# Six adjacency blocks built ahead from the end of layer zero, and layer two's residual sums in turns with the split of the silu rows

## The chip, the core and the metric

The kernel runs on one core of one Trainium2 chip. The metric is the time of one execution on the device in microseconds. The engines are TensorE (PE, with its weight loads as PEld), VectorE (DVE), ScalarE (ACT), GpSimd (POOL) and SyncE (SP), which issues most of the transfers. Each has a queue of its own, works it off in order, and waits at semaphores for the others.

## The reference

Four graph layers over 3125 nodes of 128 features and 53125 edges, each followed by a residual sum and a normalisation of the rows:

```python
edge_index = jnp.stack([src, dst])
x = _layernorm(x + _L0(x, src, dst, ...))                        # attention, 4 heads
x = _layernorm(x + _L1(x, edge_index, W))                        # relu((H + segment_sum(H[src], dst)) @ W)
x = _layernorm(x + _L2(x, edge_index, edge_attr_4, ...))         # silu messages, edge weights, update net
x = _layernorm(x + _L3(x, edge_index, edge_type_64, ...))        # (x[src] + rel) @ W_msg.T, mean over dst
```

Layer one needs, for each node, the sum of its neighbours' rows. That is a product with the adjacency matrix, whose entry (source, destination) is the number of edges between the two.

## The kernel before

Nodes are cut into NB = 25 blocks of 128. Layer zero walks over NT = 650 tiles of 128 edges in NBATCH = 109 batches of six: TensorE gathers source rows through one-hot matrices, VectorE weights them (L1767), TensorE scatters them to the destinations (L2500). ScalarE copies the sums of a block from PSUM (L1194), and VectorE normalises.

Layer one makes the adjacency out of the same one-hot matrices. Its steps are numbered s = 0 to 174, s = q x 25 + b: b is a source block, q one of seven groups of destination blocks, four blocks (512 columns) wide for q = 0 to 3 and three (384 columns) for q = 4 to 6. For each step:

- VectorE writes one-hot rows of the sources into one of SBUF = 6 places (`set_hots`, L1950). The one-hot matrices of the destinations come from memory in chunks of five blocks (`hots_load`, L774), four chunks at a time in `big` and `XT`.
- TensorE multiplies them, `build(s)` (L2581 to L2591), into one of four PSUM banks (`adj_bank`). From s = 4 on it waits until the bank is free, that is until copy s-4 has been made.
- ScalarE copies the block to one of XBUF = 4 places of `adjf` in fp32r (L1286), once `apply1(s-4)` has released that place. We call it the wide copy. A second copy as bytes goes to memory for layer three: for s % 5 in 1, 3 VectorE makes it from `adjf` (L1965), for the others ScalarE makes it from PSUM (L1289).
- TensorE multiplies the rows of the nodes, in two parts `XH` and `XL`, with `adjf`: `apply1(s)` (L2611).

The order on TensorE is written out by hand: build(0), build(1), then for each even s build(s+2), build(s+3), apply1(s), apply1(s+1). Waits are on counts, so a queue stands at its first wait that isn't met. The waits that matter here are these (before, in `build` and in ScalarE's loop):

```python
if s >= 4:
    pe.wait_ge(adjf_cp, s - 3)          # wide copy s-4 made
    act_copied(pe, s - 4)               # ScalarE's byte copies up to s-4 made
...
act.wait_ge(adj_mm, s + 1)              # build(s) done
if s >= XBUF:
    act.wait_ge(applied, s - XBUF + 1)  # apply1(s-4) done
```

Between the layers, TensorE turns the counts of neighbours (`rc_tr`, L2552), ScalarE copies them (`crow`, L1269), SyncE stores them (L786), reads them back as a broadcast of 1600 KB (L788), and only then issues the loads of chunks two and three. The rows of layer one's input are scaled by ScalarE (L1227) and VectorE, and parted into `XH` (ScalarE, L1255) and `XL` (VectorE, L1983).

Layer two begins with dense products in seven banks of four blocks: messages (Wagg), residual (Wres, semaphore `xr`) and the first part of the update net (`upx`, L2670). The silu rows `T1` are parted into three bf16 parts for the gathers: ScalarE copies the top part (L1246), VectorE takes the rest (L1944), ScalarE copies the middle part (L1249), VectorE takes the low part (L1940). Then VectorE adds the residual to the bias (L2006), which frees the banks in PSUM for `upx`, and ScalarE adds the bias to `upx` (L1308). The gathers (`gather2`, L2688) wait for all seven.

Of the kernel before, what the change touches and what calls it, by code (L numbers as in the profile page):

```python
# [13 lines left out]
P = 128  # L14
F = 128
# [32 lines left out]
def gnn_kernel(nc, ins, out):  # L48
# [113 lines left out]
    def up2_at(i):  # L162
        return up_at(i) + 4

# [45 lines left out]
    with ctx:  # L210
# [491 lines left out]
        def _(sp):  # L702
# [77 lines left out]
            for r in range(3):  # L780
                sp.wait_ge(hots_out[r], hots_stored(r))
# [13 lines left out]
            for n in range(BANKS * NCK):  # L795
                q, c = n // NCK, n % NCK
                if n == 0:
                    sp.wait_ge(hots_wide, NBATCH)
                    hots_load(2)
                    hots_load(3)  # L800
# [10 lines left out]
                if c == 1 and q:  # L811
                    rel_store(q - 1)
# [213 lines left out]
        def _(act):  # L1026
# [169 lines left out]
            for k in range(NBATCH):  # L1196
# [5 lines left out]
                own_values(k)  # L1202
                if k + 1 < NBATCH:
                    hots_widened(k + 1, 0)
# [37 lines left out]
            def split(n, src, ready):  # L1242
                for i in range(BANKS + 1):
                    if i < BANKS:
                        ready(i)
                        C.copy(XP[:, nodes(i), 0, :], src[:, nodes(i), :]).then_inc(xp_top, 1)  # L1246
                    if i:
                        act.wait_ge(xp_rest, BANKS * n + i)
                        C.copy(XP[:, nodes(i - 1), 1, :], AG[:, cols(i - 1)].rearrange("p (b f) -> p b f", f=F)).then_inc(xp_mid, 1)  # L1249

            C.copy(SLc[:, 1, :, :], SLc[:, 0, :, :]).then_inc(pairs_ready, 1)

# [3 lines left out]

            for h in range(2):
                deviations(1, h)
            act.wait_ge(scale_ready, 1)
# [9 lines left out]
            C.copy(crow[:, :], bank(7)[0:NB, 0:P]).then_inc(rc_cp, 1)  # L1269
# [8 lines left out]
            for q in range(BANKS):  # L1278
                w = even_width(q)
                for b in range(NB):  # L1280
                    s = q * NB + b
                    act.wait_ge(adj_mm, s + 1)
                    if s >= XBUF:
                        act.wait_ge(applied, s - XBUF + 1)
                        dve_copied(act, s - XBUF)
                    C.copy(adjf[:, s % XBUF, 0:w], adj_bank(s)[:, 0:w]).then_inc(adjf_cp, 1)  # L1286
                    if not by_dve(s):
                        adj_free(act, s)
                        C.copy(adj_slot(s), adj_bank(s)[:, 0:w]).then_inc(adj_act, 1)  # L1289
                    if q == 0 and b % 2 == 0 and HBANK - 1 + b // 2 < BANKS:  # L1290
                        round_rows(1, HBANK - 1 + b // 2)
                    if q and b == 9:
                        rel_rows(q - 1)
# [9 lines left out]
            split(1, T1, lambda i: act.wait_ge(silu2, i + 1))  # L1303
            act.wait_ge(rows2_out, 16 * BANKS)
            for i in range(BANKS):
# [149 lines left out]
        def _(dve):  # L1455
# [196 lines left out]

            dve.wait_ge(pool_consts, 8)
# [97 lines left out]
            for k in range(NBATCH):  # L1751
# [11 lines left out]
                if k + 1 < NBATCH:  # L1763
# [5 lines left out]
                                va[:, :, :, F:ROW0].unsqueeze(4).to_broadcast([P, a, n // a, H, FH]), ALU.mult).then_inc(vals_ready, 1)  # L1769
                for i in range(BANKS):  # L1770
# [125 lines left out]
            def normalise(n, dst, *steps):  # L1896
# [40 lines left out]
            def split(n, src):  # L1937
                def low(i):
                    dve.wait_ge(xp_mid, BANKS * (n - 1) + i + 1)
                    V.tensor_tensor(XP[:, nodes(i), 2, :], AG[:, cols(i)].rearrange("p (b f) -> p b f", f=F), XP[:, nodes(i), 1, :], ALU.subtract).then_inc(xp_low, 1)  # L1940

                for i in range(BANKS):
                    dve.wait_ge(xp_top, BANKS * n + i + 1)
                    V.tensor_tensor(AG[:, cols(i)].rearrange("p (b f) -> p b f", f=F), src[:, nodes(i), :], XP[:, nodes(i), 0, :], ALU.subtract).then_inc(xp_rest, 1)  # L1944
# [901 lines left out]
```

## Time and profile before

| | us |
|---|---|
| median of 3 runs | 1089.12 |
| lowest and highest | 1088.42, 1090.14 |
| profiled execution | 1089.84 |
| its span from first to last instruction | 1088.0 |
| TensorE busy | 1002.6 (92%) |
| VectorE busy | 861.1 (79%) |
| ScalarE busy | 691.3 (64%) |
| GpSimd busy | 218.2 (20%) |

The profile is one execution. A view by stretch gives each engine's busy time in a part of the span, and the clock that TensorE was granted as a share of 2.4 GHz. A view in order of time gives start, duration, engine, line and operation, out<-in, a count of merged instructions, and in brackets the idle time of the engine before it with what ended it. PE's durations overlap, since products are pipelined: the distance from start to start tells how long one holds the engine.

### The profile page before, as it was taken

Reading aid. Unit: us, or ns where it says so; the run is one execution under the profiler, and the core shown is the slowest. Engines: PE = TensorE matmul, PEld = TensorE weight load, DVE = VectorE, ACT = ScalarE, POOL = GpSimd, SP = SyncE. Lnnn points to the kernel's source line nnn. Section 1 sums busy time; section 2 is a strip of 40 time slices with the busy share of each in tenths; the row PEclk is TensorE's granted clock in tenths of the full one; section 3 lists DMA queues with packets and bytes.
Section 4 is the critical chain, followed back from the end, with each engine's and each line's share of the span. In section 5 each row is a group of like instructions: output and inputs, shape, how many; then the busy total and the mean of one; then the engine's idle time right before and its main releaser. Section 6 shows DMA issues by size and latency. Waiting matters only on the chain.

```text
span 1088.0 us, 27899 instructions
## 1 busy us (share of the span) xinstructions
PE 1002.6 (92%) x10463; PEld 874.7 (80%) x10463; DVE 861.1 (79%) x1934; ACT 691.3 (64%) x1489; POOL 218.2 (20%) x260
## 2 busy tenths in 40 slices
PE   3798979699999999995999999779999999989997
PEld 3343557599999999995788889669999999976775
DVE  6875999988998989987766677788787888766754
ACT  3467765454555555456888888577677776776554
POOL 4501340000000000000000000126666666610000
PEclk9899999899999999997999999889999999999998
DMA  6000020366767677752866564235444445334232
GB/s 159 1 2 1 4 68 3 121 207 225 238 215 225 222 238 227 204 175 72 292 195 193 172 201 141 82 104 140 138 136 129 131 131 139 109 112 124 69 99 82
DMA packets 86925, 150.38 MB, mean 138 GB/s; under 512 B 14524, under 2 KB 58375, under 8 KB 86557
## 3 DMA queue, kind: packets, MB, share of 16 engines
q1 hardware_dynamic: 65609, 116.01, 35.9%
q10 hardware_dynamic: 16122, 22.16, 5.7%
q0 software_dynamic: 5056, 10.36, 3.9%
q8 instruction: 88, 1.44, 0.5%
q14 instruction: 50, 0.40, 0.1%
HBM read 112.56 MB, written 35.94 MB: 136 GB/s over the span
## 4 chain that ended last, share of the span: by engine, by line
PE 81%; DVE 10%; ACT 4%; issue 3%; DMA 2%; POOL 0%; POOLq 0%; DVEq 0%; SPq 0%; ACTq 0%
PE PS L2500 14%; PE PS L2705 14%; PE PS L2488 11%; PE PS L2688 8%; PE PS L2611 7%; PE PS L2791 6%; PE PS L2581 3%; PE PS L2588 3%; PE PS L2326 2%; PE PS L2339 2%; DVE ring L1659 2%; DVE vo L1663 2%; PE PS L2403 2%; ACT X L1227 1%; PE PS L2357 1%
## 5 line engine op out<-in xcount | busy, mean ns | idle before, releaser
L1151 ACT CAST vo<-XT 128x768 f32<-128x768 bf16 (+1 forms) x218 | 180.3, 827 | 163.7 <-PE PS L2705 64.2
L984 POOL DMA_INDIRECT XT<-tab,ring x158 | 159.9, 1012 | 113.5 <-PE PS L2705 60.2
L2500 PE MATMUL PS<-vo 128*128 128x133 f32 x1300 | 175.9, 284 | 1.2 <-ACT vo L1151 1.2
L2500 PEld LDWEIGHTS PS<-vo 128*128 128x128 f32 x1300 | 157.2, 191 | 1.4 <-issue 1.4
L2488 PE MATMUL PS<-kp,ring 128*128 128x132 bf16 x1950 | 146.7, 221 | 3.2 <-DVE ring L1631 1.7
L2705 PE MATMUL PS<-vo 128*128 128x128 f32 x984 | 132.8, 279 | 0.0
L2488 PEld LDWEIGHTS PS<-kp,ring 128*128 128x128 bf16 x1950 | 125.6, 97 | 5.4 <-DVE ring L1631 1.8
L1641 DVE TENSOR_TENSOR XT<-iotab,XT 128x768 bf16<-128x768 bf16 (+1 forms) x218 | 120.0, 551 | 3.2 <-DMA hots_d<-XT 1.5
L2705 PEld LDWEIGHTS PS<-vo 128*128 128x128 f32 x984 | 118.9, 191 | 3.0 <-issue 2.4
L2490 PE MATMUL PS<-SDP,ring 128*128 128x12 bf16 x650 | 110.2, 170 | 0.0
L1286 ACT CAST adjf_r<-PS 128x512 fp32r<-128x512 f32 (+1 forms) x175 | 92.4, 550 | 25.4 <-PE PS L2581 23.6
L1631 DVE TENSOR_SCALAR ring<-ring,pcolm 128x1664 bf16<-128x1664 bf16 x146 | 91.2, 652 | 18.9 <-PE PS L2688 15.5
L1767 DVE TENSOR_TENSOR vo<-PS,vo 128x768 f32<-128x768 f32 (+1 forms) x109 | 103.2, 947 | 0.7 <-ACT vo L1201 0.5
L2107 DVE TENSOR_TENSOR vo<-PS,EWS 128x640 f32<-128x640 f32 (+2 forms) x109 | 82.3, 755 | 27.1 <-PE PS L2688 26.9
L2688 PE MATMUL PS<-kp,ring 128*128 128x128 bf16 x1476 | 99.9, 219 | 0.8 <-ACT big L1308 0.8
L965 POOL IOTA ring<- 128x650 int32 x1 | 0.8, 759 | 477.5 <-PE PS L2588 477.5
L2688 PEld LDWEIGHTS PS<-kp,ring 128*128 128x128 bf16 x1476 | 91.3, 98 | 2.3 <-ACT big L1308 1.0
L1950 DVE TENSOR_TENSOR ring<-IN,SLc 128x768 bf16<-128x768 bf16 x182 | 91.4, 550 | 0.0
L2791 PE MATMUL PS<-adjf_r,xh_r 128*128 128x512 f32 (+1 forms) x175 | 70.6, 404 | 7.2 <-DVE adjf_r L2255 3.4
L2611 PE MATMUL PS<-adjf_r,xh_r 128*128 128x512 f32 (+1 forms) x175 | 72.9, 417 | 0.0
L1103 ACT ACTIVATE kp<-PS 128x512 f32<-128x512 f32 x104 | 57.6, 608 | 23.0 <-PE PS L2326 22.1
L2611 PE MATMUL PS<-adjf_r,xl_r 128*128 128x512 f32 (+1 forms) x175 | 65.3, 373 | 0.0
(350 smaller groups left out, 2008.6 us busy)
## 6 DMA issues: line engine op xcount, KB each, us to landing
ring<-rows_d SPq DMA_DIRECT2D x146, 416.0 KB, 5.8
hots_d<-XT ACTq DMA_DIRECT2D x108, 192.0 KB, 4.7
big<-hots_d SPq DMA_DIRECT2D x10, 640.0 KB, 5.3
XT<-hots_d SPq DMA_DIRECT2D x10, 640.0 KB, 4.8
adj_d<-ring SPq DMA_DIRECT2D x20, 320.0 KB, 2.4
big<-hots_d SPq DMA_DIRECT2D x8, 480.0 KB, 4.4
adj_d<-ring SPq DMA_DIRECT2D x15, 240.0 KB, 2.1
ring<-adj_d SPq DMA_DIRECT2D x11, 320.0 KB, 3.0
```

Of the source, the lines that this page charges most:

```text
L984: G.indirect_dma_start(far_rows[:, f % FBUF, :], None, tab[2], bass.IndirectOffsetOnAxis(ap=far_row[:, t:t + 1], axis=0)).then_inc(far_in[ ...
L1151: C.copy(ohd[:, k % 3, 0:n, :], ohb[:, k % 3, 0:n, :]).then_inc(hots_wide, 1)
L1286: C.copy(adjf[:, s % XBUF, 0:w], adj_bank(s)[:, 0:w]).then_inc(adjf_cp, 1)
L1641: V.tensor_tensor(ohb[:, k % 3, 0:n, :].rearrange("p t (h d) -> p t h d", d=2), iotab[:, :].rearrange("p (h d) -> p h d", d=2).unsqueeze(1 ...
L1767: V.tensor_tensor(va[:, :, :, 0:F].rearrange("p a i (h f) -> p a i h f", h=H), gathered(k, 0, F).rearrange("p a i (h f) -> p a i h f", h=H ...
L2488: T.matmul(PS[:, to:to + ROW0], ohT[:, 0, h % OBUF, l * P:(l + 1) * P], KP[:, source(t), part, :], start=part == 0, stop=part == 2)
L2490: T.matmul(PS[:, to + ROW0:to + ROW0 + 3 * H], ohT[:, 1, h % OBUF, l * P:(l + 1) * P], SDP[:, t // JN, :, :].rearrange("p t h -> p (t h)") ...
L2500: T.matmul(bank(6 + b % 2)[:, 0:VW], ohd[:, k % 3, i, :], vals[:, k % 3, i, :], start=j == 0, stop=j == JN - 1).then_inc(scattered, 1)
L2611: o = T.matmul(to[:, 0:w], xs[:, b, :], adjf[:, s % XBUF, 0:w], start=b == 0 and part == 0, stop=False, skip_group_check=True)
L2688: o = T.matmul(PS[:, to:to + F], ohT[:, 0, h % OBUF, l * P:(l + 1) * P], XP[:, source(t), part, :], start=part == 0, stop=part == 2)
L2705: T.matmul(bank(6 + q % 2)[:, (b % 4) * P:(b % 4 + 1) * P], rows_of(k, i, t), ohd[:, k % 3, i, :], start=j == 0, stop=j == JN - 1).then_in ...
L2791: o = T.matmul(to[:, 0:w], xs[:, b, :], adjf[:, s % XBUF, 0:w], start=b == 0 and part == 0, stop=False, skip_group_check=True)
```

## The change

One piece is layer one's start and the distance between building and applying. The one-hot rows of blocks 0 to 5 and of the diagonal are written in layer zero's last batches, from batch 103 on (EARLY_HOTS, AHEAD = 6). TensorE builds blocks 0 to 3 as soon as layer zero's last sums are copied, turns the counts into bank 4 instead of bank 7, builds blocks 4 and 5, and from then on builds s+6 and s+7 before it applies s and s+1. XBUF and the four PSUM banks are as before. ScalarE makes the first four wide copies before the normalisation and its byte copies of them between the standard deviations and the scaling of the rows. SyncE issues the loads of chunks zero and one earlier; those of chunks two and three stay behind `crow`. VectorE's byte copies follow set_hots at a distance of six instead of four, and the relation sums move three blocks later.

The other piece is in layer two: VectorE's residual sums (L2006) stand in turns with its split steps, and ScalarE's `upx` copies in turns with its own.

```diff
+    EARLY_HOTS = HT * (NU - 1) // BT - 3
+    AHEAD = 6
...
             for r in range(3):
-                sp.wait_ge(hots_out[r], hots_stored(r))
+                sp.wait_ge(hots_out[r], 16 * len(range(r, (len(even(0)) * JN - 1) // BT + 1, 3)))
             extra_load(0)
             hots_load(0)
             hots_load(1)
...
+            def block_wide(s):
+                w = even_width(s // NB)
+                act.wait_ge(adj_mm, s + 1)
+                if s >= XBUF:
+                    act.wait_ge(applied, s - XBUF + 1)
+                    dve_copied(act, s - XBUF)
+                C.copy(adjf[:, s % XBUF, 0:w], adj_bank(s)[:, 0:w]).then_inc(adjf_cp, 1)
+
+            def block_byte(s):
+                if not by_dve(s):
+                    adj_free(act, s)
+                    C.copy(adj_slot(s), adj_bank(s)[:, 0:even_width(s // NB)]).then_inc(adj_act, 1)
+
+            for s in range(XBUF):
+                block_wide(s)
             for h in range(2):
                 deviations(1, h)
+            for s in range(XBUF):
+                block_byte(s)
             act.wait_ge(scale_ready, 1)
...
             act.wait_ge(rc_tr, 1)
-            C.copy(crow[:, :], bank(7)[0:NB, 0:P]).then_inc(rc_cp, 1)
+            C.copy(crow[:, :], bank(4)[0:NB, 0:P]).then_inc(rc_cp, 1)
...
+            for i in range(BANKS + 3):
+                if i < BANKS:
+                    act.wait_ge(silu2, i + 1)
+                    C.copy(XP[:, nodes(i), 0, :], T1[:, nodes(i), :]).then_inc(xp_top, 1)
+                if 0 < i <= BANKS:
+                    act.wait_ge(xp_rest, BANKS + i)
+                    C.copy(XP[:, nodes(i - 1), 1, :], AG[:, cols(i - 1)].rearrange("p (b f) -> p b f", f=F)).then_inc(xp_mid, 1)
+                if i >= 3:
+                    hidden_start(i - 3)
...
+                if k == EARLY_HOTS:
+                    dve.wait_ge(pairs_ready, 3)
+                    set_hots(0, NB, ohx[:, 0, :])
+                if 0 <= k - EARLY_HOTS < AHEAD:
+                    set_hots(0, k - EARLY_HOTS, ohs[:, k - EARLY_HOTS, :])
...
-                    set_hots(0, NB, ohx[:, 0, :])
...
-                    set_hots(q, b, ohs[:, s % SBUF, :])
-                    if s >= 4:
-                        adj_copy(s - 4)
+                    if s >= AHEAD:
+                        set_hots(q, b, ohs[:, s % SBUF, :])
+                    if s >= AHEAD:
+                        adj_copy(s - AHEAD)
...
+            for i in range(BANKS + 2):
+                if i < BANKS:
+                    rest_of(i)
+                if 0 < i <= BANKS:
+                    low_of(i - 1)
+                if i >= 2:
+                    residual(i - 2)
...
-                if s == 3:
-                    pe.wait_ge(rc_cp, 1)
+                if s == 0:
+                    pe.wait_ge(vals_ready, NBATCH)
+                    pe.wait_ge(sums_cp, NB)
...
-            build(0)
-            build(1)
+            for s in range(XBUF):
+                build(s)
+            pe.wait_ge(cnt_ready, 1)
+            T.transpose(bank(4)[0:NB, 0:P], rc[:, :], ident[:, :]).then_inc(rc_tr, 1)
+            for s in range(XBUF, AHEAD):
+                build(s)
             for s in range(0, NS, 2):
-                for n in (s + 2, s + 3):
+                for n in (s + AHEAD, s + AHEAD + 1):
                     if n < NS:
                         build(n)
                 for n in (s, s + 1):
```

TensorE at the start of layer one, before: the end of build(2), build(3), and the first apply. `rc_cp` is the count copied by ScalarE.

```order
L2588 MATMUL PS<-ring,big 128x64 x4
L2581 MATMUL PS<-big,ring 128x128 [waits rc_cp,ohs_ready]
L2581 MATMUL PS<-big,ring 128x128 x3
L2584 MATMUL PS<-big,ring 128x128
L2588 MATMUL PS<-ring,big 128x64 x4
L2611 MATMUL PS<-adjf_r,xh_r 128x512 [waits adjf_cp,xp_rest]
L2611 MATMUL PS<-adjf_r,xl_r 128x512
```

The same place now: build(3), the transposed counts, build(4), build(5) and the first product of build(6); build(7), apply1(0) and apply1(1) come behind it.

```order
L2607 MATMUL PS<-big,ring 128x128 [waits ohs_ready]
L2607 MATMUL PS<-big,ring 128x128 x3
L2610 MATMUL PS<-big,ring 128x128
L2614 MATMUL PS<-ring,big 128x64 x4
L2653 MATMUL PS<-ident,rc 25x128 [waits cnt_ready]
L2607 MATMUL PS<-big,ring 128x128 [waits adj_act,adjf_cp,ohs_ready]
L2607 MATMUL PS<-big,ring 128x128 x3
L2614 MATMUL PS<-ring,big 128x64 x4
L2607 MATMUL PS<-big,ring 128x128 [waits adj_act,hots_got1,adjf_cp,ohs_ready]
```

The first apply stands behind eight builds instead of four, and the builds from the fifth on wait for ScalarE's copies (`adjf_cp` the wide ones, `adj_act` the byte ones).

ScalarE between the layers, before: `SLc` is copied, then the normalisation, the count row and the first wide and byte copy.

```order
L1251 COPY SLc<-SLc 128x728
L1223 ACT_TABLE_LOAD
L1223 ACTIVATE rstd<-mb,eps 128x16 [waits var_ready]
L1223 ACTIVATE rstd<-mb,eps 128x9 [waits var_ready]
L1227 ACTIVATE X<-big,shift,rstd 128x128 [waits scale_ready]
```

ScalarE between the layers, now:

```order
L1260 CAST adjf_r<-PS 128x512 [waits adj_mm] x4
L1231 ACT_TABLE_LOAD
L1231 ACTIVATE rstd<-mb,eps 128x16 [waits var_ready]
L1231 ACTIVATE rstd<-mb,eps 128x9 [waits var_ready]
L1265 CAST ring<-PS 128x512 x2
L1235 ACTIVATE X<-big,shift,rstd 128x128 [waits scale_ready]
```

Four wide copies stand ahead of the normalisation and two byte copies inside it; the copy of `SLc` is in layer zero's batch 101.

ScalarE in layer two's preparation, before (L1246 top part, L1249 middle part, L1308 the update net's bias):

```order
L1246 CAST kp<-big 128x4x128 [waits silu2]
L1249 CAST kp<-big 128x4x128 [waits xp_rest]
L1246 CAST kp<-big 128x128 [waits silu2]
L1249 CAST kp<-big 128x4x128 [waits xp_rest]
L1249 CAST kp<-big 128x128 [waits xp_rest]
L1308 ACTIVATE big<-PS,bu 128x512 [waits xp_rest,upx,rows2_out]
```

The same place now (L1322 top, L1325 middle, L1317 bias):

```order
L1325 CAST kp<-big 128x4x128 [waits xp_rest]
L1317 ACTIVATE big<-PS,bu 128x512 [waits xp_rest,upx,rows2_out]
L1322 CAST kp<-big 128x4x128 [waits silu2]
L1325 CAST kp<-big 128x4x128 [waits xp_rest]
L1317 ACTIVATE big<-PS,bu 128x512 [waits xp_rest,upx]
```

The bias steps moved from behind all copies to one behind each pair of copies, and each waits for TensorE (`upx`).

## Rows read from the trace of the kernel before

**Rows 1.** Busy time by stretch: PE, PEld, DVE, ACT, POOL, granted clock, DMA share, GB/s.

```profile
499.80:510.10 10.30, 0.59 (x2) 0.20 (x2) 8.49 (x40) 6.74 (x15) 0.00 (x0) 0.76 0.32 113
524.80:680.00 155.20, 155.07 (x1618) 132.12 (x1619) 108.18 (x241) 127.40 (x277) 0.76 (x1) 1.00 0.63 193
```

**Rows 2.** Order of time, TensorE, the first block and build(10).

```profile
509.80 0.39 PE L2560 MATMUL PS<-zeros 1*128 1x256 bf16 x1 [5.33 <-DVE ring L1950]
...
524.93 0.39 PE L2581 MATMUL PS<-XT,ring 128*128 128x128 bf16 x4 [0.17 <-DMA XT<-hots_d]
```

**Rows 3.** Order of time, TensorE and ScalarE, a pair of steps with 512 columns.

```profile
601.30 0.48 PE L2611 MATMUL PS<-adjf_r,xh_r 128*128 128x512 f32 x1
601.31 0.59 ACT L1289 CAST ring<-PS 128x512 uint8<-128x512 f32 x1
...
601.78 0.60 ACT L1286 CAST adjf_r<-PS 128x512 fp32r<-128x512 f32 x1
601.85 0.39 PE L2611 MATMUL PS<-adjf_r,xh_r 128*128 128x512 f32 x1
...
602.08 0.40 PE L2611 MATMUL PS<-adjf_r,xl_r 128*128 128x512 f32 x1
...
602.31 0.41 PE L2581 MATMUL PS<-big,ring 128*128 128x128 bf16 x4
...
602.76 0.59 ACT L1286 CAST adjf_r<-PS 128x512 fp32r<-128x512 f32 x1 [0.38 <-PE PS L2581]
602.79 0.41 PE L2581 MATMUL PS<-big,ring 128*128 128x128 bf16 x4
...
603.24 0.48 PE L2611 MATMUL PS<-adjf_r,xh_r 128*128 128x512 f32 x1
```

**Rows 4.** The same view, a pair of steps with 384 columns.

```profile
674.00 0.36 PE L2581 MATMUL PS<-big,ring 128*128 128x128 bf16 x3
...
674.36 0.35 PE L2581 MATMUL PS<-big,ring 128*128 128x128 bf16 x3
674.40 0.86 ACT L1286 CAST adjf_r<-PS 128x384 fp32r<-128x384 f32 x2 [0.18 <-PE PS L2581]
...
674.70 0.42 PE L2611 MATMUL PS<-adjf_r,xh_r 128*128 128x384 f32 x1
...
675.13 0.34 PE L2611 MATMUL PS<-adjf_r,xh_r 128*128 128x384 f32 x1
...
675.14 0.50 ACT L1289 CAST ring<-PS 128x384 uint8<-128x384 f32 x1
...
675.31 0.33 PE L2611 MATMUL PS<-adjf_r,xl_r 128*128 128x384 f32 x1
...
675.48 0.36 PE L2581 MATMUL PS<-XT,ring 128*128 128x128 bf16 x3
```

**Rows 5.** One line's instructions, ScalarE's wide copy: shortest, median, longest ns, forms.

```profile
L1286 ACT CAST adjf_r<-PS x175: 473/585/623, 514.5 to 679.0; 128x512 fp32r<-128x512 f32 x100, 128x384 fp32r<-128x384 f32 x75
```

**Rows 6.** The page's group of set_hots; order of time, ScalarE's scaling and SyncE's load.

```profile
L1950 DVE TENSOR_TENSOR ring<-IN,SLc 128x768 bf16<-128x768 bf16 x182 | 91.4, 550 | 0.0
...
506.29 3.18 ACT L1227 ACTIVATE X<-big,shift,rstd 128x128 f32<-128x128 f32 x8 [0.53 <-DVE shift L1916]
...
516.32 0.98 SPq L774 DMA_DIRECT2D XT<-hots_d  x2
```

**Rows 7.** Order of time, layer two's preparation: VectorE's residual sums, last bias steps, first gather.

```profile
715.43 3.87 DVE L2006 TENSOR_TENSOR big<-PS,bu 128x512 f32<-128x512 f32 x7
...
723.60 0.94 ACT L1308 ACTIVATE big<-PS,bu 128x512 f32<-128x512 f32 x2 [0.17 <-PE PS L2670]
...
724.60 3.19 PE L2688 MATMUL PS<-kp,ring 128*128 128x128 bf16 x54 [0.82 <-ACT big L1308]
```

**Rows 8.** Busy time by stretch, columns as in rows 1: TensorE with pauses, and idle.

```profile
147.00:160.00 13.00, 9.23 (x107) 8.41 (x104) 11.44 (x16) 7.55 (x22) 9.10 (x11) 1.00 0.48 137
711.30:716.10 4.80, 0.00 (x0) 0.00 (x0) 4.80 (x11) 3.10 (x7) 0.00 (x0) 0.71 0.00 0
```

More of the change, by code:

```diff
@@ L798, in _ @@
                     sp.wait_ge(hots_wide, NBATCH)
+                    for r in range(3):
+                        sp.wait_ge(hots_out[r], hots_stored(r))
                     hots_load(2)
@@ L810, in _ @@
                     extra_load(q + 1)
-                if c == 1 and q:
+                if c == 2 and q:
                     rel_store(q - 1)
@@ L1202, in _ @@
                 own_values(k)
+                if k == EARLY_HOTS - 2:
+                    C.copy(SLc[:, 1, :, :], SLc[:, 0, :, :]).then_inc(pairs_ready, 1)
                 if k + 1 < NBATCH:
@@ L1240, in copy_xt @@
                     C.copy(XT[:, cols(i)], PS[:, cols(i)]).then_inc(xt_act, 1)
[L1242 to L1251, printed above, removed]
             def round_rows(n, i):
@@ L1281, in _ @@
                     s = q * NB + b
-                    act.wait_ge(adj_mm, s + 1)
                     if s >= XBUF:
[L1284 to L1289, printed above, removed]
+                        block_wide(s)
+                        block_byte(s)
                     if q == 0 and b % 2 == 0 and HBANK - 1 + b // 2 < BANKS:
                         round_rows(1, HBANK - 1 + b // 2)
-                    if q and b == 9:
+                    if q and b == 12:
                         rel_rows(q - 1)
@@ L1302, in _, with hidden_start @@
                 C.activation(T1[:, nodes(i), :], NX[:, nodes(i), :], ACT.Silu).then_inc(silu2, 1)
-            split(1, T1, lambda i: act.wait_ge(silu2, i + 1))
-            act.wait_ge(rows2_out, 16 * BANKS)
-            for i in range(BANKS):
+            def hidden_start(i):
+                if i == 0:
+                    act.wait_ge(rows2_out, 16 * BANKS)
                 act.wait_ge(upx, i + 1)
@@ L1651, in _, with set_hots @@
             FIRST = [h for h in units_at(0) if HT * h < 2 * BT]
+            def set_hots(q, j, buf):
+                V.tensor_tensor(buf.rearrange("p (k n b) -> p k n b", k=3, b=4), IN1[:, :, :].rearrange("p (k n) b -> p k n b", k=3),
+                                SLc[:, :, j, 4 * q:4 * q + 4].unsqueeze(2).to_broadcast([P, 3, NREL, 4]), ALU.is_equal).then_inc(ohs_ready, 1)
             dve.wait_ge(pool_consts, 8)
@@ L1935, in copy_xt @@
                     V.tensor_copy(XT[:, cols(i)], PS[:, cols(i)]).then_inc(xt_dve, 1)
[L1937 to L1944, printed above, removed]
-                    if i:
-                        low(i - 1)
-                low(BANKS - 1)
-            def set_hots(q, j, buf):
-                V.tensor_tensor(buf.rearrange("p (k n b) -> p k n b", k=3, b=4), IN1[:, :, :].rearrange("p (k n) b -> p k n b", k=3),
-                                SLc[:, :, j, 4 * q:4 * q + 4].unsqueeze(2).to_broadcast([P, 3, NREL, 4]), ALU.is_equal).then_inc(ohs_ready, 1)
-            dve.wait_ge(pairs_ready, 3)
             normalise(1, X)
@@ L2605, in apply1 @@
                     pe.wait_ge(crel_cp, q - 1)
+                if b == 0 and q == 1:
+                    pe.wait_ge(rc_cp, 1)
                 if q == 0:
```

20 lines of the change are left out of this document (12 added, 8 removed).

## The prediction

> **What bounds the kernel now.** I read the page's busy times, then the table of busy time by stretch, then the order of time around the three places that the diff touches. TensorE bounds it. From 524.8 to 680.0 us, which is nearly all of layer one's product with the adjacency, TensorE is busy 155.07 of 155.20 us at full clock [rows 1]. That stage has no slack: whatever makes TensorE wait there lengthens the kernel. The slack lies beside it: 10.3 us with almost no TensorE work between layer zero and the first block [rows 1, 2], and layer two's preparation, where the projections end 0.8 us before the first gather [rows 7].
>
> In the full stage each pair of steps is build(s+2), build(s+3), apply1(s), apply1(s+1). With 512 columns a pair takes 601.30 to 603.24, 1.94 us: the first apply 0.55, the second 0.46, the builds 0.48 and 0.45 [rows 3]. With 384 columns it takes 674.00 to 675.48, 1.48 us: the second build 0.34, the first apply 0.43 [rows 4]. ScalarE's copies never hold TensorE up here, because the block that is to be copied was applied long ago.
>
> **The distance of six.** This is the term that decides. Nothing is added to TensorE's work, but the builds stand six blocks ahead of the applies instead of two, and both rings keep four places. Follow an even n. build(n) waits until block_wide(n-4) has emptied its PSUM bank. block_wide(n-4) waits until apply1(n-8) has released its place in `adjf`. With distance two TensorE has applied up to n-3 when it reaches build(n): five applies lie between apply1(n-8) and it. With distance six it has applied up to n-7: apply1(n-8) is the last but one instruction group on the same queue, and only apply1(n-7), 0.46 us, stands between. So a turn TensorE, ScalarE, TensorE comes into every pair, and the engine that was full waits in it.
>
> The turn, 512 columns, counted from the point where apply1(n-8) has been issued:
> - its last product ends 0.17 us later (602.08 + 0.40 against the next group's 602.31), and ScalarE starts 0.04 us after a product's end (602.31 + 0.41, then 602.76) [rows 3]: 0.21 us;
> - block_wide(n-4), then block_byte(n-4): ScalarE goes from one to the next in 0.47 us (601.31 to 601.78) [rows 3]: 0.94 us for both;
> - block_wide(n-3), which build(n+1) waits for, whole: 0.60 us [rows 3];
> - back to TensorE: 0.06 us (the last activation ends at 723.60 + 0.94, the gather starts at 724.60) [rows 7];
> - build(n+1), the second of its pair, 0.45, and apply1(n-6), the first of its, 0.55 us [rows 3], and the turn is closed.
>
> That is 0.21 + 0.94 + 0.60 + 0.06 + 1.00 = 2.81 us. Of the five kinds of pair by s % 5 (bytes of s % 5 in 0, 2, 4 are ScalarE's, the rest VectorE's), four have one byte copy in this chain and one has two, which makes 3.28 us. Where the one byte copy belongs to the second block it stands behind block_wide(n-3), and the sum is the same. The mean is (4 x 2.81 + 3.28) / 5 = 2.90 us, 0.96 us over 1.94. It holds from build 10 to build 99, 45 pairs: **43.2 us**.
>
> With 384 columns: 0.16 + 0.04 (675.31 + 0.33 against 675.48), copies 0.37 apart (674.40 with two copies, then 675.14), the wide copy 0.49 (the two take 0.86), 0.06, build 0.34, apply 0.43 [rows 4]. That is 0.20 + 0.74 + 0.49 + 0.06 + 0.77 = 2.26 us, 2.63 with two bytes, mean 2.33: 0.85 us over 1.48. Blocks 100 to 174 (100 wide copies of 512 columns, 75 of 384 [rows 5]) are 37.5 pairs: **31.9 us**. TensorE waits for about a third of the stage (1 - 1.94 / 2.90); VectorE and the loads have more room than before, so nothing else becomes late.
>
> At a boundary of two column groups TensorE's extra products partly fill a wait, and ScalarE's two small copies of the relation sums, hidden now, come into the chain. I set these off against each other and keep 3 us both ways.
>
> **The start of layer one.** The six set_hots of the first blocks, 0.55 us each [rows 6], and the one for the diagonal move into the last batches of layer zero, where VectorE has idle time between batches; only the last two stand before the last sums, up to 1.1 us on the chain into the normalisation, and one (0.5) leaves it. Builds 0 to 3 now run at 500 us instead of from 509.80 [rows 2]. But two byte copies (0.94 us) stand in front of ScalarE's row scaling, which had 0.53 us of idle time before 506.29 [rows 6]. Together `crow` comes about 1.1 - 0.5 + 0.94 later, 1.5 us. That matters through SyncE's queue: the loads of chunks two and three still stand behind `crow`'s store, and the first one ends the wait at 524.93 [rows 2, 6]. build(10) needs it. In the order of before TensorE has then done applies 0 to 7; in the new order apply1(4) stands behind build(10), so only 0 to 3. The head start therefore ends in a longer wait for the same transfer: 1.5 us later, and four applies owed, which at the end, at 384 columns, cost about 4 x 0.39 = 1.6 us. **+3.1 us**; bounds 0 (crow not later, the applies inside later waits) to 6. The early load of chunks zero and one costs nothing: their queue waits for nothing that is late.
>
> **Layer two.** The seven residual sums (715.43, 3.87 us [rows 7]) are spread among the split steps. VectorE's total is the same, so its last sum still ends near 719.3. A last narrow projection and activation need about 1 us more, so the gather can start at 720.3 at the best, 4.3 us before 724.60 [rows 7]. But on ScalarE the activation of bank i-3 now stands ahead of the silu copy of bank i+1, which VectorE's next split step waits for: projection, activation, copy, three VectorE steps of 0.55 to 0.6 and the handoffs close a round of about 4.4 us for two banks. From a first sum at 710.8 that gives the last activation at 722.8, or 724.5 if the clock is low in it. I take **-1.5 us**; bounds -4.3 and 0.
>
> The rest (`SLc`'s copy, the later place of relation rows, PSUM bank 4 for the count row) lies beside busy TensorE: 0.
>
> **Sum.** 1089.84 (profiled) + 43.2 + 31.9 + 3.1 - 1.5 = 1166.5. The median of the runs is 0.7 below the profiled one: 1165.8, say 1166 us.
>
> **Rivals.**
> A, the clock also falls. At half clock a pair costs TensorE at most twice 1.94, 3.9 us, against 2.90; half of the stage so is about (3.9 - 2.90) x 22 + (2.96 - 2.33) x 19 = 34 us more: 1200. Against it: from 147 to 160 us TensorE worked with pauses, busy 9.23 of 13 us, and the clock stayed full (mean 1.00), while it fell in the idle time from 711.3 to 716.1 (mean 0.71) [rows 8]; the new stage has work for 1.94 of 2.90 us and 1.48 of 2.33, in pauses of about half a microsecond. The Trainium skill (TensorE: Matmul & The Clock Gate, section "A second HAM failure mode: psum-queue depth-cycling") says that short idle times between groups of products, while PSUM banks are cycled in each iteration, make the clock swing between its two levels; by that rule this rival is the likelier one, by the rows the full clock. 6%.
> B, the turn is shorter by one copy, because ScalarE's byte copies find a place outside the chain: 0.47 x 45 + 0.37 x 37.5 = 35 us less, 1131. Against it: the queue is in order and build(n) waits for the byte of n-4 or its predecessor. 5%.
> C, faster: the turn is hidden as it was before. It decides at one point, whether a wide copy and a byte copy fit behind one apply of 0.46 us; they need 1.3. If they did, TensorE would stand five builds and two applies further when `crow` is written, 5 x 0.48 + 2 x 0.46 = 3.3 us, and with layer two's 1.5 the time is 1084. For it speaks only that ScalarE is busy 127.40 of 155.20 us [rows 1], so it has room in sum. 2%. With the late load (+3.1 - 1.5) the same hidden turn gives 1091, no difference: 2%.
>
> **How the numbers follow.** Forecast 85%, A 6%, B 5%, C 2% and 2%. Within the forecast a tenth of a microsecond more or less in each of the 82 turns is 8 us, and the other bounds are 3 and 4 us: 1153 to 1181, with 80% of the chance inside. 0.2%, 2.2 us, is about what a measurement of this kernel tells from no change: faster 0.02, same 0.02, slower 0.96.
>
> **What would show it.** Right: TensorE's builds wait for the wide or byte copy, some 0.9 us a pair from the first block to the last, the stage from build 10 to the last apply lasts about 230 us instead of 155, granted clock 1.00 in it, ScalarE's wide copies waiting for applies rather than builds; the load of chunk two lands at about 526 with TensorE idle before it. Wrong: pairs still near 1.94 us (C), 2.4 (B) or a clock under 0.9 there (A); a first gather more than 4 us nearer to the end of layer one than now.

## The result, and the profile after

The changed kernel takes 1178.24 us, median of 4 runs (1175.88 to 1181.61). The kernel before, run beside it, takes 1089.63 us (1088.42 to 1091.07). The ratio is 1.081, with a 95% interval of 1.080 to 1.083. The forecast was 1166, with a range of 1153 to 1181: slower, by the mechanism named, 12 us too little.

The profiled execution of the changed kernel took 1175.88 us, with a span of 1174.1 against 1088.0. Four moments, read from TensorE's order of time in both traces, divide the 86.1 us between them:

| stretch | before, us | after, us | difference |
|---|---|---|---|
| start to build(10) | 524.93 | 527.49 | +2.6 |
| build(10) to the last products of layer one (first `identr` product) | 155.2 | 239.2 | +84.1 |
| from there to layer two's first gather | 44.5 | 42.2 | -2.3 |
| first gather to the end | 363.4 | 365.2 | +1.8 |

So the full stage has nearly the whole loss. This is the table of busy time by stretch of the changed kernel, with the columns of [rows 1]: first TensorE's wait before build(10), then a short stretch behind it, then the stage whole and one piece of it.

```profile
523.70:527.40 3.70, 0.00 (x0) 0.00 (x0) 1.96 (x4) 1.33 (x4) 0.00 (x0) 1.00 0.93 303
528.20:531.60 3.40, 3.14 (x20) 2.18 (x17) 1.13 (x4) 1.48 (x3) 0.00 (x0) 0.55 1.03 358
531.60:766.00 234.40, 171.92 (x1595) 131.09 (x1596) 106.39 (x237) 128.55 (x276) 1.67 (x3) 1.00 0.40 121
...
600.00:660.00 60.00, 43.77 (x409) 32.39 (x406) 26.16 (x57) 32.53 (x64) 0.00 (x0) 1.00 0.41 125
```

Before, TensorE was busy 155.07 of 155.20 us [rows 1]; now it is busy 171.92 of 234.40, at the same granted clock of 1.00. (The busy time grew though the work didn't: before a pause the end of the last product, 0.16 us, is no longer covered by a next one, which is one reason why the waits below add up to less than 84 us.) Its waits in the stage, summed from 527 to 767 us (engine, line, what it waited for: us in total, times, longest), and the group of ScalarE's wide copy from the page (busy, mean ns, idle time before it and its releaser):

```profile
PE PS L2607 <- ACT ring L1265: 48.6, 80, 0.8
PE PS L2607 <- issue: 7.7, 26, 0.3
PE PS L2607 <- DVE ring L1673: 5.9, 14, 1.1
PE PS L2607 <- DMA XT<-hots_d: 3.8, 1, 3.8
```

```profile
L1260 ACT CAST adjf_r<-PS 128x512 fp32r<-128x512 f32 (+1 forms) x175 | 92.8, 547 | 114.5 <-PE PS L2607 100.1
```

Eighty waits of builds (L2607) for ScalarE's byte copy (L1265), and ScalarE's wide copy (L1260) in its turn 100.1 us idle for TensorE: each waits for the other. One such turn in the order of time, the columns being start, duration, engine and line, with idle time and releaser in brackets. It answers to [rows 3].

```profile
644.72 0.39 PE L2607 MATMUL PS<-big,ring 128*128 128x128 bf16 x4 [0.83 <-ACT ring L1265]
...
645.17 0.41 PE L2607 MATMUL PS<-big,ring 128*128 128x128 bf16 x4
...
645.62 0.47 PE L2639 MATMUL PS<-adjf_r,xh_r 128*128 128x512 f32 x1
645.93 0.39 PE L2639 MATMUL PS<-adjf_r,xl_r 128*128 128x512 f32 x1
646.16 0.40 PE L2639 MATMUL PS<-adjf_r,xh_r 128*128 128x512 f32 x1
646.41 0.58 ACT L1260 CAST adjf_r<-PS 128x512 fp32r<-128x512 f32 x1 [1.34 <-PE PS L2607]
646.89 0.59 ACT L1265 CAST ring<-PS 128x512 uint8<-128x512 f32 x1
647.36 0.60 ACT L1260 CAST adjf_r<-PS 128x512 fp32r<-128x512 f32 x1
647.62 0.39 PE L2607 MATMUL PS<-big,ring 128*128 128x128 bf16 x4 [0.83 <-ACT ring L1265]
...
648.07 0.24 PE L2607 MATMUL PS<-big,ring 128*128 128x128 bf16 x1
...
648.58 0.47 PE L2639 MATMUL PS<-adjf_r,xh_r 128*128 128x512 f32 x1
```

The first apply's last product ends at 646.32 (645.93 + 0.39), ScalarE starts at 646.41, its byte copy ends at 647.48, TensorE's first build starts at 647.62 and its second at 648.07. From build to build it is 2.90 us, where [rows 3] had 1.94. The bracket at ScalarE's wide copy names the build L2607 as what it waited for, but that build had been done long ago; the wide copy waits for the apply as well, and starts 0.09 us behind its end. Such a bracket has to be read with the ends of the rows around it.

### The profile page after: what moved, and what is told of

Read it like the earlier page. It is cut to its first block and busy times, and to the rows that moved or that the text cites. A ratio compares the mean times of both kernels' runs of the same rounds, so it can differ in the third digit from the quotient of the medians.

```text
span 1174.1 us, 27901 instructions
## 1 busy us (share of the span) xinstructions
PE 1018.9 (87%) x10463; PEld 872.3 (74%) x10463; DVE 861.4 (73%) x1934; ACT 692.7 (59%) x1489; POOL 218.6 (19%) x260
## 5 line engine op out<-in xcount | busy, mean ns | idle before, releaser
L1157 ACT CAST vo<-XT 128x768 f32<-128x768 bf16 (+1 forms) x218 | 180.3, 827 | 165.3 <-PE PS L2737 64.1
L1260 ACT CAST adjf_r<-PS 128x512 fp32r<-128x512 f32 (+1 forms) x175 | 92.8, 547 | 114.5 <-PE PS L2607 100.1
L1660 DVE TENSOR_TENSOR XT<-iotab,XT 128x768 bf16<-128x768 bf16 (+1 forms) x218 | 119.9, 551 | 1.6 <-DMA hots_d<-XT 0.8
L1975 DVE CAST ring<-adjf_r 128x512 uint8<-128x512 f32 (+1 forms) x70 | 27.8, 397 | 124.6 <-ACT adjf_r L1260 124.6
L1650 DVE TENSOR_SCALAR ring<-ring,pcolm 128x1664 bf16<-128x1664 bf16 x146 | 91.4, 654 | 18.8 <-PE PS L2720 15.7
```

The source lines that it names most:

```text
L1157: C.copy(ohd[:, k % 3, 0:n, :], ohb[:, k % 3, 0:n, :]).then_inc(hots_wide, 1)
L1660: V.tensor_tensor(ohb[:, k % 3, 0:n, :].rearrange("p t (h d) -> p t h d", d=2), iotab[:, :].rearrange("p (h d) -> p h d", d=2).unsqueeze(1 ...
```

## Experiments

Ten kernels were run. Beside each median stands the ratio to the kernel before, which ran on the same chip beside them (1090.05 us, 1089.75 and 1090.05 in the three groups).

### Distance four instead of six

```diff
-    AHEAD = 6
+    AHEAD = 4
```

> The changed kernel with AHEAD = 4 instead of 6, everything else kept (builds 0 to 3 early, the early set_hots, layer two's new order). Theory (the turn TensorE, ScalarE, TensorE comes from the distance of six on rings of four places): between apply1(n-8) and build(n) TensorE now has apply1(n-7), two builds and two applies, some 2.4 us of work against a turn of about 1.3 to 1.8 us on ScalarE, so nothing waits: stage from build 10 to the last apply about 156 us, pairs 1.94 us. Total 1089.6 + 2.6 (crow and with it the load of chunk two later) + 0.8 (two applies owed at that load) - 1.5 to -2.4 (layer two) = about 1091, 1088 to 1094. Rival 1 (the waits come from the moved set_hots, the new bank or the early blocks, not from the distance): stays above 1150. Rival 2 (each step away from distance two costs in proportion): about 1130.

Measured: 1092.99 us (10 runs, 1091.71 to 1094.74), ratio 1.0029 (1.0017 to 1.0041). One number takes 85 us off. Busy time by stretch of this kernel, and its build(10):

```profile
524.00:681.00 157.00, 157.00 (x1620) 133.45 (x1621) 106.81 (x237) 126.99 (x277) 1.09 (x3) 0.99 0.62 191
```

```profile
524.00 0.42 PE L2607 MATMUL PS<-XT,ring 128*128 128x128 bf16 x4 [3.17 <-DMA XT<-hots_d]
```

The stage has no wait, so the distance is the cause, and it doesn't act in proportion: at four the turn is hidden, at six it isn't. The 2.9 us left over the kernel before are no turns. The start has one part of them, with the wait of 3.17 us for chunk two; layer two's part is told below.

### The distance alone, in the kernel before

```diff
-            build(0)
-            build(1)
+            for s in range(6):
+                build(s)
             for s in range(0, NS, 2):
-                for n in (s + 2, s + 3):
+                for n in (s + 6, s + 7):
...
-                    if s >= 4:
-                        adj_copy(s - 4)
+                    if s >= 6:
+                        adj_copy(s - 6)
```

(The small copies moved with it as in the changed kernel: places 8, 12 and 2 instead of 5, 9 and 1; so did VectorE's parting of the later rows into `XL`.)

> The kernel before with the distance alone: TensorE builds six blocks ahead, VectorE's byte copies and the small copies stand where the changed kernel has them for that distance; start of layer one, bank 7 for the count row and layer two as before. Theory (distance): stage from build 10 to the last apply 84 us longer as in the changed kernel, four applies owed at the load of chunk two (+1.6), crow not later: 1089.6 + 84 + 1.6 = 1175, 1166 to 1184. Rival (the loss sits in the early start and its queue order): under 1110.

Measured: 1177.61 us (4 runs, 1175.29 to 1178.81), ratio 1.080 (1.078 to 1.083). The distance alone gives the whole loss, with layer zero's end and layer two as before. Together with the first run this excludes the moved set_hots, the new bank and the early blocks as a cause.

### ScalarE's byte copies out of the turn

```diff
         def by_dve(s):
-            return s % 5 in (1, 3)
+            return True
```

> The changed kernel with all byte copies on VectorE (by_dve true for every block), distance six kept. Theory (the turn's length is the sum of ScalarE's copies in it): 1.2 byte copies on average leave each turn, 0.47 us with 512 columns and 0.37 with 384: 0.56 x 45 + 0.44 x 37.5 = 42 us less, 1136 us, 1126 to 1146; pairs about 2.46 us with 512 columns, all alike. VectorE then has 2 x (0.55 + 0.43) = 1.96 us a pair. Rival (VectorE's set_hots, six places in a ring that TensorE empties six ahead, sets the pace): VectorE's added work lengthens the pair, 1178 or more.

Measured: 1134.39 us (4 runs), ratio 1.040 (1.038 to 1.043); 44 us less than the changed kernel, expected were 42. Distance six is kept, VectorE has more work than in the changed kernel, and yet the time falls. TensorE in the order of time:

```profile
622.93 0.39 PE L2607 MATMUL PS<-big,ring 128*128 128x128 bf16 x4 [0.35 <-ACT adjf_r L1260]
625.36 0.39 PE L2607 MATMUL PS<-big,ring 128*128 128x128 bf16 x4 [0.34 <-ACT adjf_r L1260]
```

The pair is 2.43 us, and it waits for the wide copy now: summed from 527 to 724 us TensorE's builds wait 19.7 us for it and 3.1 us for VectorE's one-hot rows. The turn's length is the sum of ScalarE's copies in it plus the handoffs, as the prediction had it; VectorE's ring of `ohs` is not what sets the pace.

### Distance six, one block at a time

```diff
-            for s in range(0, NS, 2):
-                for n in (s + AHEAD, s + AHEAD + 1):
+            for s in range(NS):
+                for n in (s + AHEAD,):
                     if n < NS:
                         build(n)
-                for n in (s, s + 1):
+                for n in (s,):
```

> The changed kernel, distance six kept, but TensorE's steps go one by one, build(s+6), apply1(s), instead of two builds and two applies. Theory (a chain TensorE, ScalarE, TensorE that closes over the queue order): now build(n-1) and apply1(n-7), 0.95 us, stand between apply1(n-8) and build(n), and the chain advances two steps in 0.24 + 0.47 + 0.60 + 0.14 + 0.45 + 0.55 = 2.45 us where the block's byte copy is ScalarE's (three blocks of five) and in 1.98 where it isn't, mean 2.26 against the 3.04 of a pair in the changed kernel (2.93 and 3.48 measured): 0.78 x 45 = 35 us less; with 384 columns 1.97 and 1.60, mean 1.82 against 2.44 (2.35 and 2.82 measured): 23 us less. 1178 - 58 = 1120, 1108 to 1135, since even and odd chains share ScalarE. Rival (only the number of blocks ahead counts against the rings of four, not the order in which they are issued): 1175 or more.

Measured: 1125.71 us (4 runs), ratio 1.033 (1.031 to 1.035): 52.5 us less than the changed kernel, expected were 58. In the order of time two steps with ScalarE's byte copy in them take the 2.45 us that were worked out:

```profile
622.43 0.39 PE L2607 MATMUL PS<-big,ring 128*128 128x128 bf16 x4 [0.29 <-ACT ring L1265]
...
623.42 0.25 PE L2607 MATMUL PS<-big,ring 128*128 128x128 bf16 x1
...
624.88 0.28 PE L2607 MATMUL PS<-big,ring 128*128 128x128 bf16 x2 [0.23 <-ACT ring L1265]
```

The number of blocks ahead is as before, and the rings have their four places. Only the order on TensorE's queue changed, and more than half of the loss went. The distance does its harm through what stands on the queue between apply1(n-8) and build(n): nothing but one apply in the changed kernel, a build and an apply here, and at distance four three applies and two builds.

### Layer two's new order alone

The kernel before with `rest_of`, `low_of`, `residual` and `hidden_start` in turns, as the diff of the change has them.

> The kernel before with the new order of layer two's split alone. In the changed kernel the stretch from the last apply to the first gather became 2.3 us shorter (42.2 against 44.5), and the stretch from the first gather to the end 1.8 us longer. Theory (a part is given back, because the load of the next row block is issued as late as before and the gathers now wait for it): first gather 2 to 2.5 us earlier, total only 0.4 to 1.0 us less, 1088.6 to 1089.2. Rival (the 1.8 us given back belong to something else in the changed kernel): total 2 to 2.5 us less, 1087.2.

Measured: 1090.48 us (12 runs, 5 rounds), ratio 1.0003 (0.9990 to 1.0015). No gain; the expected part of a microsecond isn't seen. Where it goes is read from three moments of each profiled execution, in us behind the first `identr` product of the last column group, with the duration of TensorE's last six projections (of the kernel before all fourteen stand in one group of 7.62 us):

| kernel | first gather | first scatter | last six projections |
|---|---|---|---|
| before | 44.5 | 47.7 | |
| changed | 42.2 | 47.1 | 2.23 |
| distance four (e1) | 43.2 | 48.2 | 2.23 |
| layer two alone (e3) | 44.3 | 47.7 | 3.90 |
| layer two with early one-hots (e6, below) | 42.1 | 45.3 | 2.23 |

From the first scatter to the end of the span every one of these executions takes 360.2 to 360.4 us. So the first scatter counts, and not the first gather, which the prediction looked at. In the changed kernel's profiled execution the first scatter came 0.6 us earlier, in that of e3 not at all. In the changed kernel, VectorE, SyncE's queue and TensorE:

```profile
806.79 1.20 DVE L1650 TENSOR_SCALAR ring<-ring,pcolm 128x1664 bf16<-128x1664 bf16 x2
...
807.45 4.73 SPq L744 DMA_DIRECT2D ring<-rows_d  x3
...
811.09 0.75 DVE L1650 TENSOR_SCALAR ring<-ring,pcolm 128x1664 bf16<-128x1664 bf16 x1 [3.10 <-DMA ring<-rows_d]
811.76 1.02 DVE L1660 TENSOR_TENSOR XT<-iotab,XT 128x768 bf16<-128x768 bf16 x2
...
813.80 1.58 PE L2737 MATMUL PS<-vo 128*128 128x128 f32 x12 [1.72 <-DVE vo L2134]
```

VectorE's first two one-hots of the edges (L1650) stand behind the last residual sum. The first of them frees a place for the third row block, which SyncE then loads; VectorE waits 3.10 us for it, the one-hots of destinations (L1660) stand behind that, and the first scatter at the end. In the kernel before the same wait was there, hidden behind the projections and ScalarE's copy of the slots:

```profile
723.67 0.65 DVE L1631 TENSOR_SCALAR ring<-ring,pcolm 128x1664 bf16<-128x1664 bf16 x1 [3.25 <-DMA ring<-rows_d]
725.74 1.04 DVE L1641 TENSOR_TENSOR XT<-iotab,XT 128x768 bf16<-128x768 bf16 x2 [1.42 <-ACT XT L1141]
```

The new order brings the projections forward but VectorE's last sum not, and so the load now ends last.

### The first edge one-hots early

```diff
             copy_xt(1)
+            edge_hots(0, 0, 1)
             for i in range(BANKS):
                 dve.wait_ge(mm2, i + 1)
...
+            edge_hots(1, 0, 1)
...
-            for h in units_at(0):
+            for h in units_at(0)[2:]:
                 edge_hots(h, 0, 1)
```

> The kernel of e3_before_layer2, with VectorE's first two edge one-hots of layer two put ahead of its additions of bagg and ahead of the split, where it waits for other engines (1.15 and 1.21 us). The load of the third row block, which waits for the first of them, then lands before 715 instead of 726. Theory (in e3 VectorE's third edge one-hot waits for this load, the one-hots of destinations wait behind it, and the first scatter behind them): the wait at 726.07 goes; what is next is ScalarE's copy of the slots, which ends at 726.4 in e3, so the first scatter comes 0.3 us earlier where TensorE's last projections run at the low clock (1.12 us became 3.90 for six), and 1.9 us earlier where they run at the full one: total 1090.2 or 1088.6, no more than 1091. Rival (layer two's start is bound elsewhere, the moved one-hots delay the residual sums): 1091 or more.

Measured: 1089.55 us (11 runs, 1087.3 to 1090.95), ratio 0.9996 (0.9987 to 1.0005). The wait for the load is gone and the first scatter follows the gather without one:

```profile
719.84 0.65 DVE L1641 TENSOR_SCALAR ring<-ring,pcolm 128x1664 bf16<-128x1664 bf16 x1
...
723.09 1.03 DVE L1651 TENSOR_TENSOR XT<-iotab,XT 128x768 bf16<-128x768 bf16 x2 [2.60 <-ACT XT L1141]
...
725.14 1.58 PE L2733 MATMUL PS<-vo 128*128 128x128 f32 x12
```

What ends last is ScalarE's copy of the slots (L1141), as expected, and behind it TensorE's projections. The profiled execution had the projections at the full clock and its scatter 2.4 us earlier; over all runs 0.2 us is left against the kernel before, where e3 was 0.4 above the one beside it, and neither is told from no change. This profiled execution was also the fastest of its eleven, and the clock in the projections is one thing that sets it apart from e3's: the same six take 2.2 us with a granted clock of 1.00 (this kernel) or 3.9 with 0.61 (e3). Both rows are from busy time by stretch, the first of this kernel, the second of e3:

```profile
718.00:722.00 4.00, 2.29 (x7) 1.03 (x8) 2.49 (x6) 2.54 (x6) 0.00 (x0) 1.00 0.07 27
```

```profile
720.60:725.00 4.40, 3.90 (x6) 1.60 (x6) 2.23 (x6) 1.39 (x3) 0.00 (x0) 0.61 0.37 88
```

TensorE had worked in short groups with the same waits, of up to 1.46 us, between them before either. e4 and e8 have this preparation too, and their six projections took 3.9 us like e3's. e8 differs from e7 in layer one's distance alone; its first scatter came 47.5 us behind the `identr` product, e7's 46.2. In e7 the low clock (0.57 from 712.0 to 715.6 us) fell on the four projections before, and the last six ran at 1.00 in 2.21 us. So the low stretch comes in one traced execution and not in another, and at different places, and what it costs depends on the place.

### The loads ahead of `crow`'s store

At distance four:

```diff
             hots_load(1)
+            sp.wait_ge(hots_wide, NBATCH)
+            for r in range(3):
+                sp.wait_ge(hots_out[r], hots_stored(r))
+            hots_load(2)
+            hots_load(3)
             sp.wait_ge(rc_cp, 1)
```

The same lines go from their old place behind the store.

> The kernel of e1_after_dist4 with SyncE's two loads of chunks two and three (and the waits for their data) put ahead of the wait for crow and its store. In e1 TensorE stood 3.17 us for that load (to 524.00) and then worked about 3 us at the low clock (builds and applies of 524.46 to 527.6 take 1.3 to 1.6 times as long, about 1 us). Theory (the load behind crow's store is what the early blocks run into): it lands before TensorE wants it, so 3.2 + 1.0 less: 1093.0 - 4.2 = 1088.8, 1087.5 to 1090.5, just below the kernel before. Rival (ScalarE's row scaling and rounding are late there as well, and take the wait over): 1092 to 1093, with a wait for ScalarE or VectorE of some 3 us in its place.

Measured: 1088.58 us (12 runs), ratio 0.9992 (0.9983 to 1.0002): by the medians 4.4 us less than e1 (4.1 by the ratios to the kernel before beside each), expected were 4.2. TensorE's build(10) follows its apply without a wait:

```profile
523.27 0.40 PE L2638 MATMUL PS<-adjf_r,xl_r 128*128 128x512 f32 x1
523.51 0.41 PE L2606 MATMUL PS<-XT,ring 128*128 128x128 bf16 x4
```

The same edit at distance six:

> The changed kernel, distance six kept, with SyncE's loads of chunks two and three ahead of crow's store. In the changed kernel TensorE waited 3.83 us for this load (to 527.49), and its clock was low again from 528.2 to 531.6. Theory (this wait is a term of its own beside the turns, as at distance four, where the same edit took 4.4 us off): 3.8 + 0.7 = 4.5 us less, 1173.7, 1172 to 1175.5. Rival (at distance six the turns take it over, since the blocks that stood ready are few): 1176 to 1178.

Measured: 1173.56 us (4 runs, 1171.36 to 1176.28), ratio 1.076 (1.075 to 1.078). By the medians 4.7 us less than the changed kernel, as the theory has it; but in the profiled executions build(10) comes 3.5 us earlier (counted from layer zero's last group of sums) and the stage's end only 1.9 us. The intervals of the two ratios don't overlap, so a gain is there. But this profiled execution is the slowest of its four and the changed kernel's the fastest, and from the first scatter to the end it took 362.0 us where the others in the table above took 360.3. Whether the turns take over part of the wait stays open.

### Both repairs together

On the changed kernel: TensorE four ahead (e7) or two ahead (e8), VectorE's six early set_hots kept, the loads ahead of `crow`'s store, the first two edge one-hots early, VectorE's byte copies four blocks behind again, and ScalarE's later byte copy behind `crow`:

```diff
-            for s in range(XBUF):
-                block_byte(s)
+            block_byte(0)
...
             C.copy(crow[:, :], bank(4)[0:NB, 0:P]).then_inc(rc_cp, 1)
+            for s in range(1, XBUF):
+                block_byte(s)
```

> Both repairs together, on the changed kernel: TensorE four ahead, VectorE's six early set_hots kept (so builds 4 and 5 need not wait for the seventh operation), loads of chunks two and three ahead of crow's store, ScalarE's byte copy of block 2 behind crow instead of ahead of the row scaling, the first two edge one-hots of layer two early. Theory: e1's 1093.0 less 4.2 (load), 0.5 (byte copy), 1.9 (row load of layer two at full clock) = 1086.4, 1084.5 to 1088.5, a little faster than before. Rival (the start of layer one is bound by ScalarE from 504 to 521 us, whatever TensorE has ready): 1088 to 1091.

> The kernel of e7_best_dist4 with TensorE two blocks ahead of the applies in the steady state, as before (builds 0 to 3 still early). Theory (four ahead and two ahead are alike in the full stage, and in the start only two builds, 0.9 us, are moved): 1086.4 to 1087.3, within 1.5 us of e7. Rival (the distance matters in steps even between two and four): a difference of more than 3 us to e7.

Measured: e7 1087.03 us (11 runs), ratio 0.9975 (0.9967 to 0.9984); e8 1086.68 us (9 runs), ratio 0.9972 (0.9962 to 0.9982). Both are faster than the kernel before, by 2.7 and 3.1 us, a quarter of a percent, and alike, so between two and four the distance is no matter. Part of the rival of e7 holds: at the start TensorE now waits for ScalarE, in its first apply by way of VectorE, which subtracts what ScalarE has rounded (`xh_r`).

```profile
510.37 0.80 PE L2642 MATMUL PS<-adjf_r,xh_r 128*128 128x512 f32 x1 [2.91 <-DVE xl_r L1995]
514.63 0.59 PE L2610 MATMUL PS<-big,ring 128*128 128x128 bf16 x4 [2.18 <-ACT ring L1265]
```

These are e7's first apply and build(6). ScalarE has scaling, rounding and copies without a break there, so the blocks that stood ready early can't be used sooner. From layer zero's last group of sums to the end of layer one it is 183.8 us before, 186.1 in e1, 181.6 in e5, 181.8 in e7 and 180.3 in e8: the early start is worth 2 to 3.5 us in these single executions, once nothing queues in its way.

## Why the prediction was right, and where its numbers were off

**What bounds it, and the mechanism.** Right. TensorE bounds the full stage, as its rows of before said, and the chain apply1(n-8), block_wide(n-4), block_byte(n-4), build(n) is what the trace shows. Three runs change its links one at a time, the distance, the copies in it, the queue order, and each moves the time about as worked out (85, 44 and 52 us; 87, 42 and 58 expected).

**The size of the turn** is the term that was mis-sized. 75.1 us were predicted for the 82 pairs, 84.1 were measured from build(10) on, in which 1.6 were foreseen for the owed applies. By its parts, 512 columns: end of the apply to ScalarE 0.25 us (646.32 to 646.41, plus 0.16 for the product's end behind the issue), predicted 0.21; ScalarE's copies 0.95 (646.41 to 647.36), predicted 0.94; the second wide copy 0.60, as predicted; its end to build(n+1) 0.11 (647.96 to 648.07), predicted 0.06; the rest about 1.00. That is 2.90 us. The way through build(n) is just as long (the byte copy's end at 647.48, build(n) at 647.62, build(n+1) 0.45 behind it), and the rows don't tell which of the two holds build(n+1). The way back of 0.06 was taken from the last bias activation and the first gather [rows 7]. The same two instructions give 0.06 again in the changed kernel (808.83 to 808.89), but behind the byte copies of the turn it is 0.14 each time; why these differ stays open. The prediction took another pair of instructions for the pair that hands over. A pair with one byte copy takes 2.90 to 2.96 us instead of 2.81, one with two 3.48 instead of 3.28. In the latter build(n+1) waits for the second byte copy, 0.14 us behind its end (602.94 + 0.62, then 603.70):

```profile
602.72 0.22 PE L2607 MATMUL PS<-XT,ring 128*128 128x128 bf16 x1 [0.83 <-ACT ring L1265]
...
602.94 0.62 ACT L1265 CAST ring<-PS 128x512 uint8<-128x512 f32 x1
...
603.70 0.28 PE L2607 MATMUL PS<-XT,ring 128*128 128x128 bf16 x2 [0.30 <-ACT ring L1265]
```

With 384 columns 2.35 and 2.82 were measured, 2.26 and 2.63 predicted. That is (4 x 2.93 + 3.48) / 5 = 3.04 over 2.90 in 45 pairs, 6.3 us, and 2.44 over 2.33 in 37.5 pairs, 4.1 us: together 10 us by these pairs. The stage itself is 7.4 us over the forecast: 47.7 us were added from build(10) to build(100) (669.05 - 527.49 = 141.6 against 618.78 - 524.93 = 93.9) and 36.4 behind it (97.7 against 61.3), forecast 43.2 and, with the owed applies, 33.5. The 3 us between 10 and 7.4 are of the size that the prediction left open for the boundaries of column groups; no run measured them alone. The profiled execution lies 9.4 us over the forecast's 1166.5; the other 2 us are one in the start and one in layer two. The median lies another 2.4 above that execution, where the prediction took 0.7 off. The prediction had priced an error in the turn, 8 us for a tenth of a microsecond, and its range held.

**The start.** Predicted +3.1. Counted from layer zero's last group of sums `crow` came 1.2 us later (19.19 us against 17.99), predicted 1.5. The wait for chunk two was 3.83 us with only applies 0 to 3 done, as predicted; it landed at 527.4, not at about 526. Build(10) so came 2.6 us later than before: 1.2 of it is `crow`, and 1.5 is that layer zero's last sums stood later in this execution. This isn't the change's doing: over the twelve profiled executions they lie anywhere from 495.1 to 498.1 us, the kernel before at 496.3, and the lowest and the highest both have the early blocks. Not foreseen was the clock: behind the wait, TensorE idle from 523.7 to 527.4, the granted clock was 0.55 from 528.2 to 531.6, near the lower of its two levels (1.2 of 2.4 GHz). e5 shows wait and clock together to be worth 4.4 us at distance four.

**Layer two.** Predicted -1.5 for the first gather, measured -2.3, of which the first scatter kept 0.6; in the medians of e3 nothing is left. The step that failed is the choice of the end point: "a last narrow projection and activation need about 1 us more, so the gather can start" is right for the gather, but the first scatter waited for a load that is issued behind VectorE's last sum. The row of before had that load's wait, 3.25 us of VectorE's time, and it wasn't asked what it would do once the gather moved.

**Rival A, the clock.** It fell away: granted clock 1.00 from 531.6 to 766.0 us with TensorE busy 171.92 of 234.40 us, in pauses of 0.83 us. The Trainium skill (TensorE: Matmul & The Clock Gate, section "A second HAM failure mode: psum-queue depth-cycling") has the clock swing where groups of products with short pauses cycle through PSUM banks; this stage does so in every turn, and the trace disagrees (the page's case has bf16 products of 512 columns, here builds of 128 and 64 columns and applies of 512 share the turn). **Rival B** (one copy less) fell too, but e4 gives its price, 44 us for 1.2 copies a turn, where 35 were set for one. **Rival C** had the right point from which it decides, what stands behind the apply on the queue: e9 puts one build more there, and e1 four groups more.

## What to carry to other kernels

How far one engine runs ahead is bounded by more than the places of the rings: write down, for one step in the queue's order, which instruction frees the place and how much work stands between it and the instruction that needs it; if that is less than the way over the other engine and back (here 1.3 us against 0.46), every step waits. Price such a turn by end-to-start gaps between the very instructions that hand over, in ungrouped rows, since an error of a tenth comes back in each step. Where work is brought forward, look for the second thing that the next stage needs, here a load whose issue stood behind the engine that had not become faster.

## What the runs showed of the hardware

- A handoff from ScalarE's byte copy to TensorE's product is 0.14 us, but 0.06 from the last bias activation to the first gather; from TensorE's last product of an apply to ScalarE's copy 0.09 us, both from end to start of the rows, a product's end being a modelled one.
- TensorE keeps its full clock through a stage with a pause of 0.83 us in every 2.9 us, yet was at 0.55 behind one of 3.8 us.
- The same six projections ran in 2.2 us or in 3.9 us (e6 and e3, granted clock 1.00 and 0.61) in profiled executions of kernels with the same instructions there, with the same waits of 0.7 to 1.5 us before them. Between e8 (3.88 us, 0.56) and e7 (2.21 us, 1.00, the low clock four projections earlier) the first scatter lies 1.3 us apart. No kernel has two traces, so that one kernel's time moves by this from one execution to the next isn't shown.
